# Re-timing the side stages of a 64-turn attention pipeline on one Trainium2 core

## What is computed

```python
x = x + tanh(g_xattn[0]) * L0_xattn(layernorm(x), ctx)           # 16 heads
x = x + tanh(g_ffn[0])   * L0_ffn(layernorm(x))                  # 256 -> 1024 -> 256, GELU, binarized weights
x = x + tanh(g_xattn[1]) * L1_xattn(layernorm(x), ctx, ctx, mask)
x = x + tanh(g_ffn[1])   * L1_ffn(layernorm(x))                  # fp8-quantized 256 -> 256
x = x + tanh(g_xattn[2]) * L2_xattn(layernorm(x), ctx)           # one head: softmax(ex @ eo^T) @ ctx
x = x + tanh(g_ffn[2])   * L2_ffn(layernorm(x))                  # token mixing, sigmoid(r) * (relu(k)^2 @ Wv)
x = x + tanh(g_xattn[3]) * L3_xattn(layernorm(x), ctx)
x = x + tanh(g_ffn[3])   * L3_ffn(layernorm(x))                  # a six-block local-attention stack
```

## Time and profile before

| | |
|---|---|
| runs of the kernel before | 5314.98, 5323.96, 5327.41 us (median 5323.96) |
| the profiled execution | 5316.32 us, of which its span 5315.0 us |
| TensorE busy | 4859.0 us (91%) |
| VectorE, ScalarE, GpSimd busy | 3451.0, 3125.6, 2384.0 us |
| first part | 0 to about 2365 us |
| units 2 and 3 (feed-forward of layer 0 beside attention) | 177.5 and 180.1 us |
| units 6, 7 (layer 1) and 8, 9 (layer 3), with `middle` | 252.9, 248.4, 238.0, 238.0 us |
| unit 11 (layer 3, nearly nothing beside) | 127.8 us |

### The profile page before, as it was taken

How to read it: one execution, slowest core, us unless ns; L and a number is a source line. 1 busy time by engine, 2 the same in 40 slices (tenths; PEclk the granted TensorE clock), 3 DMA queues, 4 the chain that set the end, 5 groups by cost and what they waited for, 6 DMA issues and landing times.

```text
span 5315.0 us, 92565 instructions
## 1 busy us (share of the span) xinstructions
PE 4859.0 (91%) x35528; PEld 3037.5 (57%) x35528; DVE 3451.0 (65%) x6514; ACT 3125.6 (59%) x6618; POOL 2384.0 (45%) x2290
## 2 busy tenths in 40 slices
PE   6888889988889898969999999999999999999997
PEld 2232333333334243228777777777777777777775
DVE  5756556666675747757666666666666666666663
ACT  3555545434344344547767767676767667676772
POOL 3111101101011111129767767676767677676762
PEclk8999999999999899989999999999999999999998
DMA  5322322222212213311000000000000000000000
GB/s 118 59 53 50 62 37 53 63 48 52 51 37 51 47 40 49 58 33 42 7 17 26 17 23 17 22 21 21 19 18 24 19 26 17 21 17 17 25 9 32
DMA packets 125161, 188.97 MB, mean 36 GB/s; under 512 B 18896, under 2 KB 67664, under 8 KB 124496
## 3 DMA queue, kind: packets, MB, share of 16 engines
q1 hardware_dynamic: 124720, 183.06, 15.2%
HBM read 150.09 MB, written 32.51 MB: 34 GB/s over the span
## 4 chain that ended last, share of the span: by engine, by line
PE 66%; DVE 16%; ACT 8%; issue 6%; POOL 3%; DMA 1%; SPq 0%; DVEq 0%; POOLq 0%; ACTq 0%
PE psum L1238 16%; PE psum L1285 12%; PE psum L468 4%; PE psum L433 4%; DVE maxes L656 4%; PE psum L454 3%; PE psum L1293 3%; PE psum L1326 3%; PE psum L1317 3%; PE psum L1308 2%; PE psum L415 2%; DVE sums L689 2%; PE psum L477 2%; ACT probs L834 1%; DVE psum L653 1%
## 5 line engine op out<-in xcount | busy, mean ns | idle before, releaser
L834 ACT ACTIVATE probs<-psum 128x1024 f32<-128x1024 f32 x768 | 774.0, 1021 | 612.0 <-PE psum L454 334.7
L656 DVE TENSOR_REDUCE maxes<-psum 128x1 f32<-128x1024 f32 x512 | 614.8, 1211 | 257.2 <-PE psum L433 253.9
L1615 POOL TENSOR_TENSOR stats<-stats,minus_half 128x8 f32<-128x8 f32 x384 | 655.3, 1707 | 31.9
L1285 PE MATMUL psum<-wqkv_hi,xs_hi 128*128 128x512 f32 (+1 forms) x1536 | 558.2, 363 | 71.2 <-ACT lwork L1536 54.6
L1611 POOL TENSOR_TENSOR lwork<-lwork 128x512 f32<-128x512 f32 x384 | 494.0, 1287 | 259.0 <-DVE lwork L1429 258.9
L1555 ACT ACTIVATE lprobs<-psum,small_stats,stats 128x128 f32<-128x128 f32 x1536 | 583.7, 477 | 8.6 <-DVE small_stats L1445 7.3
L1427 DVE TENSOR_TENSOR lwork<-psum,rotary 128x512 f32<-128x512 f32 x384 | 263.6, 687 | 496.2 <-PE psum L1285 440.4
L454 PE MATMUL psum<-stack 98*128 98x512 bf16 x1536 | 515.6, 392 | 68.1 <-DVE maxes L656 32.2
L433 PE MATMUL psum<-stack 96*128 96x512 bf16 x1536 | 476.9, 394 | 62.2 <-ACT probs L834 51.7
L1285 PE MATMUL psum<-wqkv_hi,xs_lo 128*128 128x512 f32 (+1 forms) x1536 | 523.5, 341 | 0.0
L1285 PE MATMUL psum<-wqkv_lo,xs_hi 128*128 128x512 f32 (+1 forms) x1536 | 523.1, 341 | 0.0
(11 more groups left out here) (224 smaller groups left out, 11583.1 us busy)
## 6 DMA issues: line engine op xcount, KB each, us to landing
stack<-k_parts SPq DMA_DIRECT2D x288, 128.0 KB
staged<-in_quads SPq DMA_DIRECT2D x144, 256.0 KB, 3.0
k_parts<-parts SPq DMA_DIRECT2D x48, 384.0 KB, 2.9
stack<-q_parts SPq DMA_DIRECT2D x288, 64.0 KB
staged<-in_w SPq DMA_DIRECT2D x54, 256.0 KB, 2.7
ctx<-in_ctxT SPq DMA_DIRECT2D x24, 512.0 KB, 4.7
q_parts<-parts SPq DMA_DIRECT2D x24, 384.0 KB, 2.3
arena<-in_ctxT SPq DMA_DIRECT2D x8, 512.0 KB, 4.5
```

What stands on the lines that cost most here:

```text
L656: ins = vector.tensor_reduce(to, pair(("M", u)), AX.XY, ALU.max)
L834: scalar.activation(probs[:, i % 6, :, :], pair(("E", u)), ACT.Exp).then_inc(S_["E_act"], 1)
L1285: ins = tensor.matmul(to, x_[:, c, b % 2, tok(tt)], w_[:, c * COLS + lo:c * COLS + hi], start=c == 0 and n == 0, stop=c == C - 1 and n == 2)
L1615: pool_step(gpsimd.tensor_tensor(st[:, 8:16], st[:, 0:8], minus_half[:, :], ALU.pow))
```

## The change

Every stage of a unit keeps its code; only its turn changes, with one stage cut in two.

- `va` moves from turns 10, 14, 18, 22 of a unit to 11, 15, 19, 23, in all units but the first; the four late `mc` of layer 1 move from 7, 11, 15, 19 to 8, 12, 16, 20.
- `ln1` of the next unit's norm moves from turn 28 to turn 30, from before the first `wo` (29) to between it and the second (31).
- In units 6 to 9 the list of `middle` is written out with explicit turns. `m1` go from 13 and 14 to 14 and 16, the loads `xl` from 15 to 16, layer 2's norm from (ln1 17, ln2 19, ln3 20) to (18, 20, 21), `ep` from 21 to 26 to 22, 24 to 28, `s2` from 27, 31, 35, 39 to 29, 33, 37, 41, `v2` from 32, 36, 40, 43 to 35, 39, 43, 45, the following norm from (47, 49, 50) to (48, 50, 51), `k2` from 53, 54 to 55, 56, `r2` from 56, 59 to 57, 58, and `rr`, `r3` from 57 to 61 to 60 to 63. Layer 1's norm goes from (0, 2, 3) to (2, 3, 4).
- `mx` (turn 51) becomes `mw` (turn 52, its first four instructions) and `mx` (turn 53, the other four).

```diff
-            put(64 * n + LAG - 10 + 4 * k if n else -1, ("va", (L, b, k)))
+            put(64 * n + LAG - 9 + 4 * k if n else -1, ("va", (L, b, k)))
...
-                put(64 * n + 7 + LAG + 4 * i - 20, ("mc", (b, 4 + i)), *([("ml", (b, 6 + i))] if i < 2 else []))
+                put(64 * n + LAG - 12 + 4 * i, ("mc", (b, 4 + i)), *([("ml", (b, 6 + i))] if i < 2 else []))
...
     def project(L, b):
         u = (L, b)
-        out = [[("cx", u)]] + norm(L, b)
+        out = list(zip((0, 2, 6, 8, 8, 10), [[("cx", u)]] + norm(L, b)))
         for j in range(7):
-            out.append([("pj", (L, b, j))] * (j < 6) + [("pk", (L, b, j - 1))] * (j > 0))
+            out.append((12 + 2 * j, [("pj", (L, b, j))] * (j < 6) + [("pk", (L, b, j - 1))] * (j > 0)))
         return out
...
     def middle(b):
-        return forward1(b) + single(b) + forward2(b)
+        steps = lambda stage, keys, at: [(t, [(stage, k)]) for t, k in zip(at, keys)]
+        norm_at = lambda L, at: steps("ln0", [(L, b)], at[0:1]) + steps("ln1", [(L, b)], at[1:2]) + steps("ln2", [(L, b)], at[2:3]) + steps("ln3", [(L, b)], at[3:4])
+        out = norm_at("f1", (0, 2, 3, 4))
+        for c, at in enumerate(((5, 6, 7, 8), (9, 10, 12, 13))):
+            out += steps("qa", [(b, c, i) for i in range(3)], at) + [(at[3], [("q1", (b, c))])]
+        out += [(14, [("m1", (b, 0))]), (16, [("m1", (b, 1)), ("xl", b)])]
+        out += norm_at("x2", (17, 18, 20, 21))
+        out += steps("ep", [(b, m, n) for m in range(C) for n in range(3)], (22, 24, 25, 26, 27, 28))
+        tiles = [(b, qt) for qt in range(QT)]
+        out += steps("s2", tiles, (29, 33, 37, 41)) + steps("s3", tiles, (30, 34, 38, 42))
+        out += steps("t2", tiles, (32, 36, 40, 44)) + steps("v2", tiles, (35, 39, 43, 45))
+        out += norm_at("f2", (46, 48, 50, 51)) + [(52, [("mw", b)]), (53, [("mx", b)])]
+        out += steps("k2", [(b, m) for m in range(C)], (55, 56)) + steps("r2", [(b, m) for m in range(C)], (57, 58))
+        out += steps("rr", [(b, m, i) for m in range(C) for i in range(2)], (60, 61, 62, 63)) + steps("r3", [(b, m) for m in range(C)], (61, 63))
+        return sorted(out, key=lambda x: x[0])
...
-                elif stage == "mx":
+                elif stage == "mw":
                     b = u
                     V.wait_ge(S_["ep_act"], at_("ep", (b, 1, 2)))
                     V.wait_ge(S_["ln3_dve"], at_("ln3", ("f2", b)))
                     for i, (mu, om) in enumerate((("mu_r", "om_r"), ("mu_k", "om_k"))):
                         for c in range(C):
                             step(vector.tensor_scalar(mixed[:, 2 * i + c, :], xn[:, c, PAD - 1:ROW - 1], sm(om, c), None, ALU.mult))
+                elif stage == "mx":
+                    b = u
                     step.join()
```

More of the change, by code:

```diff
@@ L173, in project, with spread @@
         u = (L, b)
-        out = [[("cx", u)]] + norm(L, b)
+        out = list(zip((0, 2, 6, 8, 8, 10), [[("cx", u)]] + norm(L, b)))
         for j in range(7):
-            out.append([("pj", (L, b, j))] * (j < 6) + [("pk", (L, b, j - 1))] * (j > 0))
+            out.append((12 + 2 * j, [("pj", (L, b, j))] * (j < 6) + [("pk", (L, b, j - 1))] * (j > 0)))
         return out
+    def spread(items):
+        return [(j * 62 // max(len(items), 30), x) for j, x in enumerate(items)]
     def forward0(b):
[L180 to L203, removed]
+        return spread(norm("f0", b) + [[("f0a", (b, i)), ("f0a", (b, i + 1))] for i in range(0, FF0, 2)]
+                      + [[]] + [[("f0b", (b, m))] for m in range(C)])
     def last_norm(b):
@@ L213, in first_order @@
     signs += [x for i in (0, 2, 1, 3, 4, 5, 6, 7) for x in ([], [("bS", i)])]
-    fill = {0: signs, 2: forward0(0), 3: forward0(1), 4: forward0(2), 5: forward0(3),
-            6: middle(0), 7: middle(1), 8: middle(2), 9: middle(3), 10: last_norm(0), 11: last_norm(1)}
+    fill = {0: spread(signs), 2: forward0(0), 3: forward0(1), 4: forward0(2), 5: forward0(3),
+            6: middle(0), 7: middle(1), 8: middle(2), 9: middle(3), 10: spread(last_norm(0)), 11: spread(last_norm(1))}
     put(-3, ("wl", "L0_att"))
-    turns = [(-3, x) for x in project(0, 0)]
+    turns = [(-3, x) for _, x in project(0, 0)]
     turns.insert(next(i for i, (t, x) in enumerate(turns) if ("pk", (0, 0, 2)) in x) + 1, (-3, [("st", GROUPS[0]), ("xi", 0), ("wl", "L0_o"), ("wl", "L0_ff")]))
@@ L224, in first_order @@
                 turns.append((t0, [("wl", f"L{L}_att")]))
-            turns += [(t0 + j * 24 // 12, x) for j, x in enumerate(project(L, b))]
-        items = fill.get(n, [])
-        turns += [(64 * n + j * 62 // max(len(items), 30), x) for j, x in enumerate(items)]
+            turns += [(t0 + j, x) for j, x in project(L, b)]
+        turns += [(64 * n + j, x) for j, x in fill.get(n, [])]
         turns.append((64 * n + 63, loads.get(n, [])))
```

## The result

| | before | after |
|---|---|---|
| median of the runs | 5324.29 us (5314.98 to 5327.41) | 5285.33 us (5280.84 to 5296.09) |
| profiled execution | 5316.32 us, span 5315.0 | 5287.22 us, span 5285.9 |
| last maximum of the first part | 2300.4 us | 2263.8 us |
| from there to the end of the span | 3014.6 us | 3022.1 us |

The ratio of the medians is 0.9933, 95% interval 0.9913 to 0.9952: the kernel is faster, by 39 us (0.7%) where 69 were forecast (77 against the median). In the profiled executions the first part gained 36.6 us and the second, whose instructions are the same, lost 7.5. So the first part is what has to be explained: 36.6 us against 69.

The account below looks back on a forecast made before the run. TensorE, 91% busy, bounds the kernel; only its idle and low-clock time can be had. 25 + 5 - 1 + 52 + 8 - 3.4 - 3.1 - 4 - 9.6 = 69 us off 5316.3 gives 5247; range 5204 to 5288.

Parts of the forecast that it names:

- `va`, units 2 to 5: Units 2 to 5: `va` in odd turns removes waits before `f0a`, low-clock time and waits of `M`; 25 us gained, 15 to 32.
- units 1, 10, 11: Units 1, 10, 11: `va` no longer behind `sh`, nor the last norm's `ln3` behind `va`; 5 us gained.
- `ln1` 28 to 30; unit 0: Eleven units: the wait only moves from first to second `wo`, 0, between -4 and +6; unit 0 loses 1 us.
- shifts behind `xl`: Units 6 to 9, turn 20: `E` waits for shifts queued behind loads on SyncE, 2.4 us each, 9.6 lost, 0 to 14.
- a rival of its own: Rival, chance 0.03: the wait in turn 20 halves the clock for 27 us a unit, 108 us lost; slower, 5355.
- The waits around `m1`: Units 6 to 9: bank waits of 5.5 + 3.7 us around `m1` and 7.1 of `ln1` behind `sh` go.
- the new norm chain: Layer 1's norm, units 6 to 9: `ln2` one turn behind `ln1` idles TensorE some 2 us, offset elsewhere; 0, ±2.5 each.
- The small waits that come: Units 6 to 9: new waits of `ep` behind `ln3` 3.4, first `wo` behind `ep` 3.1, `E` behind `s2` 4 us.
- The clock's 8 of 16 us: Turns 47 to 51 of units 8 and 9: a high clock would save 8 us each; 8 of the 16 credited.
- The credit for `r2`: Tail of units 6 to 9: 13.4 us of waits before `r2` go, but VectorE bounds; 7 credited, 0 to 13.
- rival (b): Chance 0.14: the clock pays more than the waits, as the low level is not granted; 28 us more gained, 5219.
- Rival (a): Chance 0.19: waits are cover, not cost, VectorE being late where quantization and `rr` stand; only 30 us gained, 5286.

Follow-up runs that it names:

- `va` alone: Kernel before with only `va` moved one turn later, to odd turns 11, 15, 19, 23, in all units but the first: 5298.25 us, one run.
- `va` at 22: Changed kernel with the fourth `va` of each unit back in turn 22 instead of 23: 5285.73 us, one run.
- `ln1` at 28: Changed kernel with the next unit's `ln1` back in turn 28 in units 0 to 5 and 10: 5288.92 us, one run.
- the kernel with `xl` in 17: Changed kernel with the loads `xl` in turn 17, behind the shifts of `sh`, instead of turn 16: 5262.06 us median, ratio 0.9889 to before.
- the runs on the norm: Changed kernel with layer 1's norm in units 6 to 9 at turns (0, 0, 2, 3) instead of (0, 2, 3, 4): 5290.36 us, one run.
- The quantization run: Changed kernel with `xl` 17, norm (0, 0, 2, 3), fourth `va` 22 outside units 6-9, `ln1` 28; then quantization earlier (4-7; 8, 9, 10, 12): 5236.41 us; last kernel tried.
- the run that brings them back: Changed kernel with three of four `v2` in each of units 6 to 9 one turn earlier, in 34, 38, 42: 5296.22 us, one run.
- the run with the old tail: Changed kernel with `mw`, `mx`, `k2`, `r2`, `rr`, `r3` in units 6 to 9 back at the spacing of the kernel before: 5303.85 us, one run.

## Why the prediction was wrong, by its steps

| step | forecast, us | measured, us | from |
|---|---|---|---|
| `va`, units 2 to 5 | -25 | -23.3 (alone: -25.5) | unit lengths, `va` alone |
| units 1, 10, 11 | -5 | +0.3 | unit lengths, `va` at 22 |
| `ln1` 28 to 30; unit 0 | 0; +1 | about 0; -0.8 (turns 23 to 35 alone: +1.7) | `ln1` at 28; unit lengths |
| units 6 to 9, turns 0 to 45, without the shifts | -24.5 | -6.0 | stretches of the kernel with `xl` in 17 |
| units 6 to 9, turn 46 to the end | -25.3 | -30.2 | the same |
| shifts behind `xl` | +9.6 | +24.0 | after against `xl` in 17 |
| first part | -69 | -36.6 | last maximum (with -0.7 ahead of unit 0) |

The forecast of turns 0 to 45 is 15.1 + 5.5 + 3.7 + 7.1 + 3.6 less the waits that come, 3.4 + 3.1 + 4; that of the rest 4.4 + 2.5 + 3.4 + 7 + 8.

**SyncE's queue: right mechanism, too small a price.** That the shifts would be stuck behind the loads was right, and in unit 8 `E` waits 2.65 where 2.4 was forecast. That was chance: the changed kernel and the runs on the norm, on `va`, on `ln1`, on `v2` and on the tail issue these transfers in the same order, and in the five runs unit 8 waits 2.9 to 4.4 us. Two things made 24 of 9.6. In units 6, 7 and 9 the waits are 3.7, 6.1 and 3.3, since the landing of the last load was taken from before (7.3) as if the queue behind it stayed as it was, and it took 8.8, 11.4 and 8.1. Over the six kernels the load takes 7.3 to 11.4 us and the four waits of `E` make 11.1 to 15.7: the changed kernel's profile is the dearest of them. And the clock was put into a rival of its own, with a chance of 0.03, as if it either held or collapsed for 27 us; it fell for some three turns each time, 8.6 us. The upper end, 14, had no clock in it.

**The waits around `m1`: the step that failed outright.** The 5.5 + 3.7 + 7.1 us of bank waits did go. But the prediction looked at `m1` and not at what feeds it. In the kernel before the second `q1` stands in turn 11, two turns ahead of the first `m1`; in the changed one in 13, one turn ahead. So TensorE now waits there (11.8 us, 8.7 of it by the row for L590). The quantization run shows this to be worth 7 to 10.6. In the same way the second `m1`, now in 16, stands right before `sh` in 17, and `sh` waits 4.5 us for it; the prediction removed the wait of `ln1` behind `sh` and did not ask what `sh` was now behind. And the new norm chain, put at 0 "between -2.5 and +2.5 each", costs 4.8 to 7.8. With 7 to 10.6, 4.5 and 4.8 to 7.8 these make 16 to 23 us, where 18.5 are missing; the 4.5 are read off the row alone, no run took them away.

**The small waits that come** were right: `wo` behind `ep` 3.5 (forecast 3.1), `wo` behind `ln1` 7.2 (7.5), `E` behind `s2` 4.1 (4), `ep` behind `ln3` 1.8, and 4.1 once the shifts no longer hold `E` up (3.4). So were those that go: `v2` has none left of 15.1, and the run that brings them back pays in full for the idle time that it adds.

**The tail** gave more than its 7 + 8. From the kernel before to the changed one turns 46 to 51 of the four units are 38.1 us shorter, and turns 52 to 63, which now hold more of the work, 8.0 longer. The clock's 8 of 16 us were worked out from the middle of turns 47 to 51 of unit 8; there the whole stretch gained 11.4 us. The credit for `r2` was halved because VectorE is busy 32.7 of 38.1 us there. But that share belongs to one order of the work. With both `r2` ahead of all `rr`, TensorE gives VectorE its input sooner (read from the order; no run shows this alone), and the matmuls of `r2` run at 612 ns instead of 792, 5.8 us that only rival (b) had counted. Against this stand 4.3 us of a new wait of `r3`.

**The plain units** lost by the turn that was overlooked: `va` in 23, the last before the reciprocals, costs 1.3 us a unit.

Rival (a) came nearest in time, 5286, but by luck: its terms add up to 39 us (15 + 19 + 5), or to 19 with all 20 of the new waits against them, and not to the 30 that it takes off. Nor does its reason hold: its VectorE bound in the tail is refuted by the run with the old tail, and what took the gain were mostly new waits, not uncovered ones. With the waits of the quantization, the norm and the shifts taken out, in the last kernel above, units 6 to 9 are 52.4 us shorter than before, where the forecast without its shifts had 49.5.

What stays open: why the load of 1 MB takes 7.3 us one time and 11.4 another in the same order (in unit 7 it is 8.8 to 9.9 in the five other kernels, so the 11.4 do not belong to the unit; other loads into the stacked operand are in flight at that time, and no run varied them), and how the 14.8 us of the tail divide.

## What to carry to other kernels

When a stage is moved, list for it and for each stage that it passes what feeds it, what it feeds and what shares its bank, and count the turns between them before and after: the gain of a removed collision is read easily from the trace, and the distances that shrink elsewhere are not, since before they showed no wait at all. On a queue that one engine issues, put the small transfer that someone waits for ahead of the bulk; the two orders here differ by one turn and 24 us. Price a new idle of TensorE at more than its length: here 15.7 us of it cost 23 to 27.

## What the hardware showed that was not expected

The time of a 4 KB transfer was set by what the same engine had issued just ahead of it: 1.6 to 1.9 us with nothing of `xl` ahead, 3.4 to 3.7 with 1 MB ahead (though another 1 MB followed 0.6 us later), 6.8 to 10.8 with 2 MB ahead. In the six kernels with 2 MB ahead, four units each, the first of the two shifts took 6.8 to 7.3 us and landed up to 3.5 us before the 1 MB load, while the second landed 0.7 to 1.1 us after that load in all 24 cases. `E` of turn 20 started 0.05 us after that second landing. By the Trainium skill, "DMA: Bandwidth & Descriptors", section "Queues, rings and completion order", the descriptors of one issuing engine are taken up in ring order on each DMA engine; the landings behind nothing, 1 MB and 2 MB agree.

A wait of 2.7 to 6.1 us on TensorE was followed by about three turns at a lower granted clock (0.69 in unit 7), and cost more in units 6 and 7 (2.8 us each) than in 8 and 9 (1.2 and 1.7): 15.7 us of idle cost another 8.6 in those turns, and turns 23 to 25 ran at 1.00 again. In the other direction, turns 47 to 51 of unit 8 went from 0.66 (0.50 in their middle) to 1.00 when the small waits around them went, more than the half that had been credited.
